# Cross-attention and quantised FFN on one core: less filler, other orders in the opening and the tail, two DMAs swapped

## The chip, the core and the metric

The kernel runs on one core of one Trainium2 chip, in one launch. The metric is the device time of that launch in microseconds. Five engines run side by side, each with its own instruction queue, and order each other by semaphores: TensorE (PE, matmuls; its weight loads are shown as PEld), VectorE (DVE), ScalarE (ACT), GpSimd (POOL) and SyncE (SP, which here only issues DMAs). Matmul results go to PSUM, which the kernel cuts into eight banks of 128 x 512 floats. All times below are microseconds unless marked ns.

## The reference, cut to what matters

```python
def layernorm(x): m = mean(x, -1); v = var(x, -1); return (x - m) / sqrt(v + 1e-5)

# x: (8, 56, 128), ctx: (8, 1500, 96); 8 heads of 64
q = (layernorm(x) @ Wq).reshape(b, n, 8, 64)
k = (ctx @ Wk).reshape(b, m, 8, 64);  v = (ctx @ Wv).reshape(b, m, 8, 64)
attn = softmax(einsum('bihd,bjhd->bhij', q, k) * 64 ** -0.5, -1)
x = x + einsum('bhij,bjhd->bihd', attn, v).reshape(b, n, 512) @ Wout + bout

def act_quant(x, clip): s = sigmoid(clip) * max(abs(x)) / 127; return clip(round(x / s), -128, 127) * s
def weight_quant(w):    s = max(abs(w), axis=1) / 127;         return clip(round(w / s), -128, 127) * s
h = layernorm(x);  xq = act_quant(h, clip_x)           # one scale for all of x
gate, up = xq @ weight_quant(w_gate).T, xq @ weight_quant(w_up).T      # 352 wide
h = act_quant(silu(gate) * up, clip_down)              # one scale for all of h
out = x + h @ weight_quant(w_down).T
```

## The kernel before

**Algebra and tiling.** The 8 x 56 tokens stand as 4 pairs of batches, 112 tokens each. For each head Wq and Wk are multiplied first (`weights_qk`, four products of two heads each), so that a query has 96 values and meets the context directly; Wv and Wout likewise. Scores are computed transposed: 125 keys by 448 queries (8 heads of 56 tokens), 12 key tiles to a batch, so 96 iterations n in all. To keep float32 accuracy with the fast matmul type, each operand is split in a high part (`_hi`) and a rest (`_lo`): the scores of a tile are three matmuls (`scores_lo` two, `scores_hi` one), and the weighted sum is three more (`weighted`), three iterations later (LAG = 3).

**Maxima.** The softmax subtracts an estimate of the maximum of each query's scores. It comes from the high parts alone: four groups (G = 4) of 112 queries against three pieces of 500 keys, so twelve chunk matmuls a batch, each followed by a VectorE maximum. The maximum goes in as a 97th row of `q_hi` against a row of -1 in `ctxT_hi`; that row is what `max_moved` counts, 16 for each of the four groups. For batch b+1 the chunks are spread over the iterations of batch b by `chunks_at`: from t = 0 to 9 the chunks 2 to 11, and at t = 10 and 11 the chunks 0 and 1 of batch b+2. For batches 1 to 7 SyncE moves the four rows by DMA (`move_max`, L243). For batch 0 the rows are transposed by small matmuls (`row`, L1136) into PSUM and copied by ScalarE (`row_copy`, L473), two groups at a time.

**The opening (L961 to L1185 on PE).** Seven filler matmuls of 512 columns, then the weight products of the first quarter, filler, the transpose of the first 112 tokens (which waits for `xn0_made`), filler, and then for each of the four groups g: two query matmuls (`first_queries`, L1141), their copy by ScalarE into `q_hi` and, in full precision, into `e_full` (`split_first_q`, L443, for groups 0 and 1; one line each for the others, L468 and L471), three chunk matmuls (`first_max_chunks`, L990) and one VectorE maximum over 1500 keys (`first_max`, L659). The banks of the chunks alternate between `p_m` and `p_n`, so group g also waits for the maximum of group g-2. The other three token pairs are normalised meanwhile, two by ScalarE (`normalised`, L455) and one by GpSimd (L319), transposed (L1168), and copied as `xnT`. The queries of heads 0 to 3 of batches 2 to 7 (`query`, L1119) stand ahead of iteration 0, those of heads 4 and 5 in iteration 0, of 6 in 1, of 7 in 2 (`LOOP_QUERIES`). Each uses the bank named in `q_banks` (L164), which must first be free: head 6 shares `p_o[1]` with head 4, head 7 shares `p_mb[1]` with head 3. ScalarE copies a query out (L483), VectorE subtracts to get `q_lo` (L668), and that frees the bank.

**Filler.** `busy(n, bank, cols)` (L963) issues n bf16 matmuls of `cols` columns on zeros, whose result nobody reads.

**DMA queues.** SyncE issues the first token pair (`x_in` pair 0), weight quarter 0, the first context in three pieces, and later all contexts. ScalarE issues the other three token pairs (L435) and weight quarter 1 (L436). VectorE has the statistics of the three pairs (L633) ahead of the rest of the first normalisation (L637 to L644) in its queue.

**The tail.** After the last weighted sum: normalise, project, second layer norm (L866 to L902), quantise x, gate and up products, quantise h, down product. The last pair's centring is ScalarE's L573; it waits for `shift2`. h has three row blocks f: VectorE quantises and casts f = 0 and 2 (L944 to L951), ScalarE f = 1 (L610, L613). The down product has one bank for each half of the tokens; each takes three matmuls, f = 0, 1, 2.

Of the kernel before, what the change touches and what calls it, by code (L numbers as in the profile page):

```python
# [4 lines left out]
F32 = mybir.dt.float32  # L5
# [42 lines left out]
def chunks_at(b, t):  # L48
    if t >= T - 2:
        return [(b + 2, t - (T - 2))] if b + 2 < B else []  # L50
    if b + 1 >= B:
        return []
    if b == 0:
        return [(1, c) for c in range(sum(FIRST_CHUNK_PLAN[:t]), sum(FIRST_CHUNK_PLAN[:t + 1]))]
    return [(b + 1, t + 2)]
# [6 lines left out]
def program(nc, x_d, ctxT_d, ctx_d, wqkT_d, wvT_d, wout_d, misc_d, wg_d, wu_d, wd_d, out_d):  # L62
    stack = ExitStack()
    with stack:
# [99 lines left out]
        q_banks = [p_s[1], p_s[0], p_mb[0], p_mb[1], p_o[1], p_mb[2], p_o[1], p_mb[1]]  # L164
        qk_banks = [p_s, p_nb[0:2], p_s, p_s]
        first_q = [bank[0:C, 2 * TOK * k:2 * TOK * (k + 1)] for bank in (p_x, p_s[1]) for k in range(2)]
        row_banks = [p_s[0], p_mb[2]]
# [66 lines left out]
        def _(sp):  # L234
# [23 lines left out]
            for p in range(1, 3):  # L258
                sp.dma_start(ctxT_hi[p][C:C + 1, :].bitcast(F32), ctxT_hi[0][C:C + 1, :].bitcast(F32)).then_inc(s.minus_copied, 16)
            wait_ctxT_lo(sp, 0)  # L260
# [27 lines left out]
        def _(pool):  # L288
# [36 lines left out]
            pool.wait_ge(s.first_q_full_made, 3)  # L325
# [105 lines left out]
        def _(act):  # L431

            act.wait_ge(s.warm_made, 1)
            act.activation(warm[:, :], warm[:, :], ACT.Exp)
            act.dma_start(x_in[:, 1:PAIRS, :], x_d[:, 1:PAIRS, :]).then_inc(s.x_loaded, 16)  # L435
            act.dma_start(wqkT[:, 1, :], wqkT_d[:, 1, :]).then_inc(qk_loaded[1], 16)  # L436
# [27 lines left out]
            normalised(1)  # L464
            normalised(2)
            act.wait_ge(s.first_q_made, G)
            for g in range(2, G):
                act.activation(pair0(q_hi, slice(2 * g, 2 * g + 2)), by_batch(first_q[g]), ACT.Copy).then_inc(s.first_q_hi_made, 1)  # L468
            act.wait_ge(s.xnT_made, 2)
            act.activation(xnT[:, TOK:ALLTOK], p_s[0][:, 0:ALLTOK - TOK], ACT.Copy, scale=-0.5).then_inc(s.xnT_copied, 1)  # L470
            act.activation(pair0(e_full, slice(4, H)), by_batch(p_s[1][0:C, 0:HQ]), ACT.Copy).then_inc(s.first_q_full_made, 1)  # L471

            def row_copy(k):  # L473

                cols = slice(2 * k * GQ, 2 * (k + 1) * GQ)
                act.wait_ge(s.row_made, k + 1)
                act.activation(q_hi[C:C + 1, 0, cols], row_banks[k][C:C + 1, cols], ACT.Copy).then_inc(max_moved[0], 32)
# [17 lines left out]
            row_copy(0)  # L495
            split_q(0)
            split_q(1)
            row_copy(1)
# [120 lines left out]
        def _(dve):  # L619
# [200 lines left out]
            for b in range(B):  # L820
# [53 lines left out]
                .then_inc(s.late_x_made, 1)  # L874
            dve.wait_ge(s.projected, PAIRS - 1)
# [3 lines left out]
            dve.wait_ge(s.ln2_step, 2 * PAIRS - 2)  # L879
            dve.tensor_scalar(veps2[:, :], mv2[:, 1:2], EPS, None, ALU.add).then_inc(s.veps2_made, 1)  # L880
            dve.tensor_scalar(shift2[:, :], mv2[:, 0:1], -0.5, None, ALU.mult).then_inc(s.shift2_made, 1)
            dve.wait_ge(s.late_x_made, 1)
            dve.reduce_max(late_max[:, :], late_x[:, :], AX.X, apply_absolute_value=True).then_inc(s.late_step, 1)
# [63 lines left out]
            dve.wait_ge(s.h_step, 3)  # L947
            dve.tensor_copy(hq[:, 0, :], h8[:, 0, :]).then_inc(s.h_quantised, 1)
            dve.wait_ge(s.h_step, 4)
            for cols in HALVES:  # L950
                dve.tensor_copy(hq[0:96, 2, cols], h8[0:96, 2, cols]).then_inc(s.h_quantised, 1)  # L951
# [10 lines left out]
        def _(pe):  # L962
# [21 lines left out]
            busy(5, p_x, 128)  # L984
# [3 lines left out]
            busy(9, p_x, 128)  # L988

            def first_max_chunks(g, pieces=range(NM)):  # L990
# [4 lines left out]
                for k in pieces:  # L995
# [7 lines left out]
            def max_chunk(b, c):  # L1003
# [6 lines left out]
                if b == 1 and c < 3:  # L1010
                    pe.wait_ge(s.last_q_lo_made, (1, 6, 4)[c])
# [107 lines left out]
            def query(h):  # L1119

                if h == 0:
                    pe.wait_ge(s.first_q_full_made, 3)
                elif h == 1:
                    pe.wait_ge(max_moved[0], 32)
                elif h < 4:
                    pe.wait_ge(s.first_max_made, G - 1)
                elif h == 4:
                    pe.wait_ge(s.first_max_made, G)
                elif h == 6:
                    pe.wait_ge(s.last_q_lo_made, 3)  # L1130
                elif h == 7:
                    pe.wait_ge(s.last_q_lo_made, 2)
# [3 lines left out]
            def row(g):  # L1136

                return pe.matmul(row_banks[g // 2][C:C + 1, g * GQ:(g + 1) * GQ], maxima[0][:, g:g + 1], ident[0:GQ, 0:GQ],
                                 start=True, stop=True)
# [12 lines left out]
            first_max_chunks(0, (0,))  # L1152
            busy(3, p_s[0], 128)
            first_max_chunks(0, (1,))
# [3 lines left out]
            first_max_chunks(0, (2,))  # L1158
# [5 lines left out]
            first_queries(3)  # L1164
            pe.wait_ge(s.xn_made, 2)
# [4 lines left out]
            first_max_chunks(2)  # L1170
            first_max_chunks(3)
            pe.wait_ge(s.xnT_copied, 2)
            row(0)
            row(1).then_inc(s.row_made, 1)
# [91 lines left out]
            pe.wait_ge(s.h_quantised, 1)  # L1266
            for k, cols in enumerate(HALVES):
                pe.matmul(y_banks[k][:, 0:ALLTOK // 2], wdT[:, 0, :], hq[:, 0, cols], start=True, stop=False)
            for k, cols in enumerate(HALVES):
                pe.wait_ge(s.h1_quantised, k + 1)  # L1270
                pe.matmul(y_banks[k][:, 0:ALLTOK // 2], wdT[:, 1, :], hq[:, 1, cols], start=False, stop=False)
                pe.wait_ge(s.h_quantised, k + 2)
# [46 lines left out]
```

## Time and profile before

| | us |
|---|---|
| median of 3 runs | 181.56 (181.48 to 181.96) |
| the profiled execution's own time | 181.43 |
| its span in the trace | 179.4 |
| busy: PE, PEld, DVE, ACT, POOL | 172.7, 142.6, 144.7, 133.8, 127.8 |
| opening, up to the first exponential of the loop (L534) | 17.43 |
| from the last matmul of the loop to the end of the last issue | 160.8 to 177.6 |

The span is the time between the first and the last thing that the hardware profiler recorded on the core; the profiled execution's own time is measured from outside and is 2.0 longer. Busy time of PE includes the filler and overlaps of pipelined matmuls, whose ends are modelled. In the timeline an entry is the start, the length, the engine, the line of the code with its operation, output and inputs and shapes, how many are merged (x3), and in brackets how long the engine was idle before it and which engine, tile and line ended that.

### The profile page before, as it was taken

How to read it: one execution, taken by the hardware profiler on the slowest of the kernel's cores; microseconds unless marked ns; L12 is line 12 of the kernel's file. 1: busy time of each engine (PE TensorE's matmuls, PEld its weight loads, DVE VectorE, ACT ScalarE, POOL GpSimd, SP SyncE). 2: the span in 40 equal slices, each digit the busy share in tenths (PEclk: the TensorE clock that was granted, in tenths of full speed). 3: DMA queues.
4: the chain of work that ended last, by engine and by line, in shares of the span. 5: the costliest groups of instructions: out<-in, count | busy, mean ns of one | idle time of the engine just before them, and what ended most of it. 6: DMA issues, size and time to landing. Idle time of an engine off the chain costs nothing.

```text
span 179.4 us, 2941 instructions
## 1 busy us (share of the span) xinstructions
PE 172.7 (96%) x889; PEld 142.6 (79%) x889; DVE 144.7 (81%) x341; ACT 133.8 (75%) x284; POOL 127.8 (71%) x135
## 2 busy tenths in 40 slices
PE   7999999999999999999999999999999999999783
PEld 2865678888888889888888898888888888898431
DVE  6596578969984896899987968999979869958784
ACT  3477989878869995778878857788877677855732
POOL 5698399989995888689987866899788675533010
PEclk9999999999999999999999999999999999999999
DMA  5767900180017000800071008100400000000001
GB/s 151 224 167 214 257 27 4 13 242 8 0 44 213 0 4 2 249 5 2 0 215 45 2 0 230 31 0 0 130 0 2 4 0 0 0 0 5 0 0 51
DMA packets 8331, 11.41 MB, mean 64 GB/s; under 512 B 4276, under 2 KB 6516, under 8 KB 8316
## 3 DMA queue, kind: packets, MB, share of 16 engines
q1 hardware_dynamic: 7900, 10.83, 22.8%
q10 hardware_dynamic: 416, 0.40, 0.7%
q8 instruction: 7, 0.11, 0.3%
q14 instruction: 8, 0.07, 0.1%
HBM read 10.97 MB, written 0.23 MB: 62 GB/s over the span
## 4 chain that ended last, share of the span: by engine, by line
PE 91%; DVE 5%; ACT 1%; issue 1%; DVEq 0%; POOL 0%; ACTq 0%; POOLq 0%
PE p_n L1057 11%; PE p_sw L1038 11%; PE p_m L1016 11%; PE p_n L1065 11%; PE p_sw L1030 11%; PE p_n L1059 11%; PE p_sw L1031 11%; PE p_n L966 2%; PE p_n L1073 1%; PE p_n L1093 1%; PE p_m L1133 1%; DVE h_flat L924 1%; PE p_m L1000 1%; PE p_n L1000 1%; PE p_sw L1133 1%
## 5 line engine op out<-in xcount | busy, mean ns | idle before, releaser
L370 POOL TENSOR_TENSOR e_lo<-e_full,e_hi 125x448 fp32r<-125x448 f32 x48 | 55.7, 1160 | 26.0 <-ACT e_full L537 24.8
L534 ACT ACTIVATE e_hi<-p_sw 125x448 fp32r<-125x448 f32 x96 | 52.2, 543 | 23.9 <-PE p_sw L1038 23.3
L675 DVE TENSOR_REDUCE chunk_max<-p_m 112x1 f32<-112x500 f32 x84 | 55.6, 673 | 16.3 <-PE p_m L1016 15.4
L1030 PE MATMUL p_sw<-q_hi,ctxT_lo 96*125 96x448 f32 x96 | 36.3, 378 | 0.0
L1057 PE MATMUL p_n<-e_hi,ctx_hi 125*128 125x448 f32 x96 | 35.5, 370 | 0.0
L1038 PE MATMUL p_sw<-q_hi,ctxT_hi 97*125 97x448 f32 x96 | 35.4, 369 | 0.0
L1065 PE MATMUL p_n<-e_lo,ctx_hi 125*128 125x448 f32 x96 | 35.1, 366 | 0.0
L1031 PE MATMUL p_sw<-q_lo,ctxT_hi 96*125 96x448 f32 x96 | 35.1, 365 | 0.0
L1059 PE MATMUL p_n<-e_hi,ctx_lo 125*96 125x448 f32 x96 | 35.0, 364 | 0.0
L690 DVE TENSOR_TENSOR e_lo<-p_n,e_hi 125x448 fp32r<-125x448 f32 x48 | 29.6, 617 | 4.0 <-ACT p_n L551 3.8
L1016 PE MATMUL p_m<-ctxT_hi,q_hi 96*112 96x500 f32 x84 | 32.2, 393 | 0.0
L348 POOL TENSOR_TENSOR ctxT_lo<-ctxT_in,ctxT_hi 96x500 fp32r<-96x500 f32 x21 | 26.6, 1266 | 1.6
L551 ACT ACTIVATE p_n<-p_sw 125x448 f32<-125x448 f32 x48 | 25.8, 537 | 2.0 <-DVE e_lo L690 1.6
L537 ACT ACTIVATE e_full<-p_sw 125x448 f32<-125x448 f32 x48 | 25.9, 539 | 0.0
L358 POOL TENSOR_TENSOR ctx_lo<-ctx_in,ctx_hi 125x384 fp32r<-125x384 f32 x24 | 24.2, 1010 | 1.9
L1065 PEld LDWEIGHTS p_n<-e_lo,ctx_hi 125*128 125x128 f32 x96 | 18.0, 188 | 4.1
L1057 PEld LDWEIGHTS p_n<-e_hi,ctx_hi 125*128 125x128 f32 x96 | 18.2, 190 | 2.7
L1031 PEld LDWEIGHTS p_sw<-q_lo,ctxT_hi 96*125 96x125 f32 x96 | 18.0, 188 | 2.1
L1038 PEld LDWEIGHTS p_sw<-q_hi,ctxT_hi 97*125 97x125 f32 x96 | 17.8, 185 | 1.8
L1030 PEld LDWEIGHTS p_sw<-q_hi,ctxT_lo 96*125 96x125 f32 x96 | 17.8, 185 | 1.8
L1059 PEld LDWEIGHTS p_n<-e_hi,ctx_lo 125*96 125x96 f32 x96 | 15.7, 163 | 3.3
L1016 PEld LDWEIGHTS p_m<-ctxT_hi,q_hi 96*112 96x112 f32 x84 | 14.8, 177 | 2.2 <-ACT ctxT_hi L491 0.4
(255 smaller groups left out, 206.2 us busy)
## 6 DMA issues: line engine op xcount, KB each, us to landing
ctx_in<-ctx_d SPq DMA_DIRECT2D x8, 504.0 KB
ctxT_in<-ctxT_d SPq DMA_DIRECT2D x7, 562.5 KB, 5.9
ctxT_in<-ctxT_d SPq DMA_DIRECT2D x3, 187.5 KB, 4.4
ctx_in<-ctx_d SPq DMA_DIRECT2D x8, 58.5 KB
q_hi<-maxima SPq DMA_DIRECT2D x28, 0.4 KB, 1.9
wout<-wout_d SPq DMA_DIRECT2D x1, 256.0 KB, 7.4
wqkT<-wqkT_d SPq DMA_DIRECT2D x1, 224.0 KB, 4.4
wvT<-wvT_d SPq DMA_DIRECT2D x1, 192.0 KB, 6.7
```

Source lines behind the costliest of these rows:

```text
L348: pool.tensor_tensor(ctxT_lo[b % 2][:, key_piece(k)], ctxT_in[b % 2][:, key_piece(k)], ctxT_hi[b % 3][0:C, key_piece(k)], ALU.subtract).th ...
L370: pool.tensor_tensor(e_lo[:, k, :], e_full[:, k, :], e_hi[:, k, :], ALU.subtract)\
L534: act.activation(e_hi[:, k, :], p_s[n % 2][0:KT, 0:HQ], ACT.Exp, scale=SCALE)\
L675: dve.reduce_max(chunk_max[:, c // NM, c % NM:c % NM + 1], p_mb[c % NM][0:GQ, 0:MC], AX.X)\
L690: dve.tensor_tensor(e_lo[:, k, :], p_x[0:KT, 0:HQ], e_hi[:, k, :], ALU.subtract).then_inc(s.lo_dve_made, 1)
L1016: pe.matmul(p_mb[k][0:GQ, 0:MC], q_hi[0:C, b, g * GQ:(g + 1) * GQ], ctxT_hi[b % 3][0:C, key_piece(k)], start=True, stop=True).then_inc(s.m ...
L1030: pe.matmul(o, ctxT_lo[b % 2][:, keys], q_hi[0:C, b, :], start=True, stop=False)
L1031: pe.matmul(o, ctxT_hi[b % 3][0:C, keys], q_lo[:, b, :], start=False, stop=False)
L1038: pe.matmul(p_s[n % 2][0:KT, 0:HQ], ctxT_hi[b % 3][:, t * KT:(t + 1) * KT], q_hi[:, b, :], start=False, stop=True)\
L1057: pe.matmul(o[:, 0:HQ], ctx_hi[b % 2][:, t, :], e_hi[:, k, :], start=(t == 0), stop=False, skip_group_check=True)
L1059: pe.matmul(o[0:C, 0:HQ], ctx_lo[b % 2][:, t, :], e_hi[:, k, :], start=False, stop=False, skip_group_check=True)
L1065: pe.matmul(o[:, 0:HQ], ctx_hi[b % 2][:, t, :], e_lo[:, k, :], start=False, stop=(t == T - 1), skip_group_check=True).then_inc(s.pv_done, 1)
```

## The change

It touches the following places:

- `chunks_at`: for batch 6, which has no batch 8 to prepare, the chunks of batch 7 run from t = 0 (two of them) to t = 8.
- `q_banks`: heads 6 and 7 swap banks, with their waits in `query` and in `max_chunk`. 
- `first_q`: groups 2 and 3 are in banks of their own (`p_s[0]` and `p_s[1]`) rather than both in `p_s[1]`.
- The rows of groups 0 and 1 of batch 0 are moved by two DMAs on SyncE's queue; `row` and `row_copy` do only groups 2 and 3.
- ScalarE's queue issues weight quarter 1 ahead of x; after the first normalisation it copies group 2, and after the second group 3.
- PE: 3 filler matmuls rather than 5, 5 rather than 9, and the 3 between the chunks of group 0 are gone; the third chunk of group 0 is ahead of the queries of group 1; the chunks of group 2 are ahead of the transposes, which now wait for `first_q_full_made` 3, since they write the bank of group 2.
- Tail on VectorE: `late_max` ahead of the last statistics, `shift2` ahead of `veps2`; the casts of h by halves of the tokens, f = 0 and 2 alternately, and PE's down product one half after the other.

```diff
return [(1, c) for c in range(sum(FIRST_CHUNK_PLAN[:t]), sum(FIRST_CHUNK_PLAN[:t + 1]))]
+    if b == B - 2:
+        return [(b + 1, c) for c in ((2, 3) if t == 0 else (t + 3,) if t + 3 < CHUNKS else ())]
     return [(b + 1, t + 2)]
...
         p_o, p_x = p_nb[0:2], p_nb[2]
-        q_banks = [p_s[1], p_s[0], p_mb[0], p_mb[1], p_o[1], p_mb[2], p_o[1], p_mb[1]]
+        q_banks = [p_s[1], p_s[0], p_mb[0], p_mb[1], p_o[1], p_mb[2], p_mb[1], p_o[1]]
         qk_banks = [p_s, p_nb[0:2], p_s, p_s]
-        first_q = [bank[0:C, 2 * TOK * k:2 * TOK * (k + 1)] for bank in (p_x, p_s[1]) for k in range(2)]
-        row_banks = [p_s[0], p_mb[2]]
+        first_q = [bank[0:C, 2 * TOK * k:2 * TOK * (k + 1)] for bank, k in ((p_x, 0), (p_x, 1), (p_s[0], 0), (p_s[1], 0))]
         g0_banks = [p_x, p_o[1]]
...
                 sp.dma_start(ctxT_hi[p][C:C + 1, :].bitcast(F32), ctxT_hi[0][C:C + 1, :].bitcast(F32)).then_inc(s.minus_copied, 16)
+            for g in range(G - 2):
+                sp.wait_ge(s.first_max_made, g + 1)
+                sp.dma_start(q_hi[C:C + 1, 0, g * GQ:(g + 1) * GQ].bitcast(F32), maxima[0][:, g:g + 1])\
+                    .then_inc(max_moved[0], 16)
             wait_ctxT_lo(sp, 0)
...
                                    ALU.subtract).then_inc(s.first_ctxT_lo_made, 1)
-            pool.wait_ge(s.first_q_full_made, 3)
+            pool.wait_ge(s.first_q_full_made, G)
...
             act.activation(warm[:, :], warm[:, :], ACT.Exp)
+            act.dma_start(wqkT[:, 1, :], wqkT_d[:, 1, :]).then_inc(qk_loaded[1], 16)
             act.dma_start(x_in[:, 1:PAIRS, :], x_d[:, 1:PAIRS, :]).then_inc(s.x_loaded, 16)
-            act.dma_start(wqkT[:, 1, :], wqkT_d[:, 1, :]).then_inc(qk_loaded[1], 16)
...
             act.wait_ge(s.shift_made, 1)
-            normalised(1)
-            normalised(2)
-            act.wait_ge(s.first_q_made, G)
             for g in range(2, G):
-                act.activation(pair0(q_hi, slice(2 * g, 2 * g + 2)), by_batch(first_q[g]), ACT.Copy).then_inc(s.first_q_hi_made, 1)
+                normalised(g - 1)
+                split_first_q(g)
             act.wait_ge(s.xnT_made, 2)
             act.activation(xnT[:, TOK:ALLTOK], p_s[0][:, 0:ALLTOK - TOK], ACT.Copy, scale=-0.5).then_inc(s.xnT_copied, 1)
-            act.activation(pair0(e_full, slice(4, H)), by_batch(p_s[1][0:C, 0:HQ]), ACT.Copy).then_inc(s.first_q_full_made, 1)
-            def row_copy(k):
-                cols = slice(2 * k * GQ, 2 * (k + 1) * GQ)
-                act.wait_ge(s.row_made, k + 1)
-                act.activation(q_hi[C:C + 1, 0, cols], row_banks[k][C:C + 1, cols], ACT.Copy).then_inc(max_moved[0], 32)
+            def row_copy():
+                act.wait_ge(s.row_made, 1)
+                act.activation(q_hi[C:C + 1, 0, 2 * GQ:HQ], p_mb[2][C:C + 1, 2 * GQ:HQ], ACT.Copy).then_inc(max_moved[0], 32)
...
             ctxT1_hi(0)
-            row_copy(0)
             split_q(0)
             split_q(1)
-            row_copy(1)
+            row_copy()
             split_q(2)
...
                 .then_inc(s.late_x_made, 1)
+            dve.wait_ge(s.late_x_made, 1)
+            dve.reduce_max(late_max[:, :], late_x[:, :], AX.X, apply_absolute_value=True).then_inc(s.late_step, 1)
             dve.wait_ge(s.projected, PAIRS - 1)
...
             dve.wait_ge(s.ln2_step, 2 * PAIRS - 2)
+            dve.tensor_scalar(shift2[:, :], mv2[:, 0:1], -0.5, None, ALU.mult).then_inc(s.shift2_made, 1)
             dve.tensor_scalar(veps2[:, :], mv2[:, 1:2], EPS, None, ALU.add).then_inc(s.veps2_made, 1)
-            dve.tensor_scalar(shift2[:, :], mv2[:, 0:1], -0.5, None, ALU.mult).then_inc(s.shift2_made, 1)
-            dve.wait_ge(s.late_x_made, 1)
-            dve.reduce_max(late_max[:, :], late_x[:, :], AX.X, apply_absolute_value=True).then_inc(s.late_step, 1)
             dve.wait_ge(s.late_pow, 2)
...
                 dve.tensor_scalar(h8[0:fn, f, :], hh[0:fn, f, 0:ALLTOK], hs[0:fn, 2:3], None, ALU.mult).then_inc(s.h_step, 1)
-            dve.wait_ge(s.h_step, 3)
-            dve.tensor_copy(hq[:, 0, :], h8[:, 0, :]).then_inc(s.h_quantised, 1)
             dve.wait_ge(s.h_step, 4)
             for cols in HALVES:
-                dve.tensor_copy(hq[0:96, 2, cols], h8[0:96, 2, cols]).then_inc(s.h_quantised, 1)
+                for f in (0, 2):
+                    fn = FT[f][1]
+                    dve.tensor_copy(hq[0:fn, f, cols], h8[0:fn, f, cols]).then_inc(s.h_quantised, 1)
             dve.tensor_tensor(hs[:, 0:1], hs[:, 1:2], wscale[:, 6:7], ALU.mult).then_inc(s.y_step, 1)
...
             weights_qk(0).then_inc(s.wqk_made, 1)
-            busy(5, p_x, 128)
+            busy(3, p_x, 128)
             pe.wait_ge(s.ident_made, 2)
...
             pe.transpose(p_mb[2][:, 0:TOK], xn[:, 0, :], ident[0:TOK, 0:TOK]).then_inc(s.xnT_made, 1)
-            busy(9, p_x, 128)
-            def first_max_chunks(g, pieces=range(NM)):
+            busy(5, p_x, 128)
+            def first_max_chunks(g):
...
                     pe.wait_ge(s.first_max_made, g - 1)
-                for k in pieces:
+                for k in range(NM):
                     if g == 1 and k == 2:
...
                 if b == 1 and c < 3:
-                    pe.wait_ge(s.last_q_lo_made, (1, 6, 4)[c])
+                    pe.wait_ge(s.last_q_lo_made, (1, 5, 4)[c])
                 done = CHUNKS * (b - 1) + c - NM + 1
...
                 if h == 0:
-                    pe.wait_ge(s.first_q_full_made, 3)
+                    pe.wait_ge(s.first_q_full_made, G)
                 elif h == 1:
-                    pe.wait_ge(max_moved[0], 32)
+                    pe.wait_ge(s.xnT_copied, 2)
                 elif h < 4:
...
                     pe.wait_ge(s.first_max_made, G)
-                elif h == 6:
-                    pe.wait_ge(s.last_q_lo_made, 3)
-                elif h == 7:
-                    pe.wait_ge(s.last_q_lo_made, 2)
+                elif h >= 6:
+                    pe.wait_ge(s.last_q_lo_made, h - 4)
                 pe.matmul(q_banks[h][0:C, TOK:ALLTOK], wqk[:, h % 2, h // 2, :], xnT[:, TOK:ALLTOK], start=True, stop=True)\
...
-                return pe.matmul(row_banks[g // 2][C:C + 1, g * GQ:(g + 1) * GQ], maxima[0][:, g:g + 1], ident[0:GQ, 0:GQ],
+                return pe.matmul(p_mb[2][C:C + 1, g * GQ:(g + 1) * GQ], maxima[0][:, g:g + 1], ident[0:GQ, 0:GQ],
                                  start=True, stop=True)
...
             busy(2, p_s[0], 128)
-            first_max_chunks(0, (0,))
-            busy(3, p_s[0], 128)
-            first_max_chunks(0, (1,))
+            first_max_chunks(0)
             pe.wait_ge(s.wqk_copied, 2)
...
             first_queries(1)
-            first_max_chunks(0, (2,))
             weights_qk(2)
...
             first_queries(3)
+            first_max_chunks(2)
+            pe.wait_ge(s.first_q_full_made, 3)
             pe.wait_ge(s.xn_made, 2)
...
             last.then_inc(s.xnT_made, 1)
-            first_max_chunks(2)
             first_max_chunks(3)
             pe.wait_ge(s.xnT_copied, 2)
-            row(0)
-            row(1).then_inc(s.row_made, 1)
             query(0)
...
-            pe.wait_ge(s.h_quantised, 1)
             for k, cols in enumerate(HALVES):
+                pe.wait_ge(s.h_quantised, 2 * k + 1)
                 pe.matmul(y_banks[k][:, 0:ALLTOK // 2], wdT[:, 0, :], hq[:, 0, cols], start=True, stop=False)
-            for k, cols in enumerate(HALVES):
                 pe.wait_ge(s.h1_quantised, k + 1)
                 pe.matmul(y_banks[k][:, 0:ALLTOK // 2], wdT[:, 1, :], hq[:, 1, cols], start=False, stop=False)
-                pe.wait_ge(s.h_quantised, k + 2)
+                pe.wait_ge(s.h_quantised, 2 * k + 2)
                 pe.matmul(y_banks[k][:, 0:ALLTOK // 2], wdT[0:96, 2, :], hq[0:96, 2, cols], start=False, stop=True)\
...
```

## Rows read from the trace of the kernel before

**Rows 1.** The page, busy time of each engine
```profile
PE 172.7 (96%) x889; PEld 142.6 (79%) x889; DVE 144.7 (81%) x341; ACT 133.8 (75%) x284; POOL 127.8 (71%) x135
```

**Rows 2.** Chain of waits, 0 to 17.5: start, us, engine, tile, line
```profile
5.60 0.62 PE p_n L966 x9
6.22 0.42 PE p_n L1144 x4
6.64 0.40 PE p_n L980 x4
...
8.40 0.23 PE p_m L1000
8.63 0.62 PE p_sw L980 x8
9.25 0.86 PE p_n L1000 x3
```

**Rows 3.** Timeline, 0 to 14: start, us, engine, line, shapes, [idle before <-releaser]
```profile
3.57 0.68 DVE L633 BATCH_NORM_STATS2 stats<-x_in 112x6 f32<-112x128 f32 x3 [0.21 <-DMA x_in<-x_in_d]
...
4.63 0.34 DVE L644 TENSOR_SCALAR xn<-x_in,mv,rstd 112x128 f32<-112x128 f32 x1
...
5.63 0.26 ACT L451 ACTIVATE xnT<-p_m 128x112 f32<-128x112 f32 x1 [0.50 <-PE p_m L987]
...
8.67 1.72 DVE L663 TENSOR_REDUCE maxima<-p_m 112x1 f32<-112x1500 f32 x1 [1.23 <-PE p_m L1000]
...
9.69 0.87 ACT L456 ACTIVATE xn<-x_in,nt,rstd 112x128 f32<-112x128 f32 x2
...
10.92 0.60 ACT L468 ACTIVATE q_hi<-p_sw 96x224 fp32r<-96x224 f32 x2 [0.37 <-PE p_sw L1144]
...
12.29 1.72 DVE L663 TENSOR_REDUCE maxima<-p_m 112x1 f32<-112x1500 f32 x1 [0.27 <-PE p_m L1000]
...
13.93 1.71 DVE L663 TENSOR_REDUCE maxima<-p_n 112x1 f32<-112x1500 f32 x1
```

**Rows 4.** DMAs: issue in the timeline, then KB and us to landing
```profile
0.92 0.39 ACTq L435 DMA_DIRECT2D x_in<-x_in_d  x1
...
1.35 0.44 ACTq L436 DMA_DIRECT2D wqkT<-wqkT_d  x1
...
q_hi<-maxima SPq DMA_DIRECT2D x28, 0.4 KB, 1.9
...
x_in<-x_in_d ACTq DMA_DIRECT2D x1, 168.0 KB, 2.6
...
wqkT<-wqkT_d ACTq DMA_DIRECT2D x1, 112.0 KB, 2.8
```

**Rows 5.** Groups by shape, filler weight loads at 4.9 and 5.9: mean ns
```profile
L966 PEld LDWEIGHTS p_n<-filler 128*128 128x128 bf16 x2 | 0.3, 152 | 0.0
...
L966 PEld LDWEIGHTS p_n<-filler 128*128 128x128 bf16 x3 | 0.2, 98 | 0.0
```

**Rows 6.** Timeline, 17 to 25, and a window (PE, PEld, DVE, ACT, POOL)
```profile
17.00 0.92 DVE L668 TENSOR_TENSOR q_lo<-p_m,q_hi 96x336 fp32r<-96x336 f32 x2 [1.36 <-ACT q_hi L483]
...
18.77 0.36 PE L1038 MATMUL p_sw<-q_hi,ctxT_hi 97*125 97x448 f32 x1
...
19.33 0.81 PE L1133 MATMUL p_n<-xnT,wqk 128*96 128x336 f32 x2 [0.20 <-DVE q_lo L668]
...
24.96 0.27 PEld L1016 LDWEIGHTS p_m<-ctxT_hi,q_hi 96*112 96x112 f32 x2 [0.36 <-ACT ctxT_hi L491]
...
21.00:23.00 2.00, 2.00 (x10) 1.65 (x9) 1.98 (x4) 2.00 (x6) 1.09 (x1) 1.00 0.92 237
```

**Rows 7.** Chain, then timeline, of the tail
```profile
165.52 0.07 DVE shift L881
...
175.64 0.45 DVE L951 CAST hq<-h 96x224 bf16<-96x224 int8 x2
...
176.44 0.81 DVE L957 SCALAR_TENSOR_TENSOR y<-p_n,hs,x1T 128x224 f32<-128x224 f32 x2 [0.28 <-PE p_n L1273]
```

## The prediction

> **What bounds the kernel now.** I read the page's busy line first: TensorE (PE) is busy 96% of the span [rows 1]. That alone says little, since filler matmuls count. The chain of waits of the opening says more [rows 2]: it stays on PE from the first filler to the loop, and nine filler matmuls stand in it just ahead of the first queries. The timeline of VectorE and ScalarE in that stretch gives the second line of work [rows 3]: four maxima of 1.72 us each, the last starting at 13.93 and so ending at 15.64, with one gap of 0.27 before the third. After it PE still runs the last row, one query and the first scores. In the loop matmuls follow each other at about 0.2 us, so the loop's length doesn't move with a shift of its start, except in its first iterations [rows 6]. In the tail every step is a dependency [rows 7].
>
> So the time moves by three things: when the fourth maximum ends, stalls in iterations 0 to 5, and steps of the tail.
>
> **Opening: the load order.** Now x is issued at 0.92 and lands 2.6 later, at 3.52; the weight quarter is issued at 1.35 and lands 2.8 later, at 4.15 [rows 4]. VectorE, idle until then, takes the three statistics at 3.57, and everything of the first normalisation stands behind them in its queue (xn0 is computed at 4.63 to 4.97) [rows 3]. Swapped, x is issued at 1.35. Bounds: it keeps its 2.6 and lands 0.43 later, or it takes the place of the second transfer (same bytes in total) and lands 0.63 later. I take 0.6. Nobody waits for the weight quarter's earlier arrival: its products come after the first queries, at 6.6. So this edit alone is a loss. The Trainium skill, DMA: Bandwidth & Descriptors, section on queues, rings and completion order, says that on each DMA engine descriptors are consumed in ring order and that ScalarE's queue is one row of rings. By that rule x would wait for the weights' bytes, the sum would go by 0.63, and the row pair above agrees in order, though no run here shows the swap.
>
> **Opening: less filler.** xn0 at 5.57 instead of 4.97. The copy of the transposed block starts 0.66 after xn0 now, with five fillers in front of the transpose; with three, and PE long free, I take 0.5: copy at 6.07 instead of 5.63, done at 6.33 [rows 3]. Before, the nine fillers held PE to 5.60+0.62=6.22 and only then came the queries [rows 2]. With five they end before 6.33, so the queries start near 6.45: the 0.6 loss has become 0.25. From there, by the chain's own pieces: queries 0.42, weight products 0.40, two fillers 0.2 (nine make 0.62), and three chunks of maxima at 0.23 each, now in one piece, without three fillers and without the second queries between: 6.45+0.42+0.40+0.2+0.69=8.16. The first maximum would start at about 8.25 instead of 8.67: gain 0.4.
>
> **Opening: the maxima.** They run at a spacing of 1.64 when fed. Second: VectorE is free at 8.25+1.64=9.9; PE, done with the chunks at 8.2, does queries 0.4, weight products 0.62 and chunks 0.86: 10.1. So 10.1 instead of 8.67+1.64=10.31. Third: now it starts at 12.29, and what it waited for is q_hi, copied only after both normalisations (9.69, 0.87 long) and after both query groups (10.92) [rows 3]. With the copy between the normalisations and only one group waited for, ScalarE can copy at about 10.5, when PE has done the third group's queries (10.1+0.42). From this copy to the maximum it takes 1.37 (10.92 to 12.29): 11.87; VectorE is free at 10.1+1.64=11.75. PE does the fourth group's queries in between, till 10.95, where the copy ends too. Gain 0.4. Fourth: 13.5 to 15.2, if its chunks are ready: the transposes now wait for the third group's full copy and the second normalisation, done by ScalarE at about 11.6 (q_hi, full copy and one normalisation from 10.5), then three transposes, which I put at the 0.4 of four query matmuls, then chunks like the 0.86: 12.9. Behind this new wait on PE stand the fourth group's chunks and all late queries, 0.6 ahead of need. If the cover goes, each 0.1 costs 0.1.
>
> **Opening: rows by DMA.** Two rows go from PE and ScalarE to SyncE's queue: four small matmuls and a 0.35 copy less, two transfers more. They wait for the first and second maxima (ending at 8.25+1.72=10.0 and 11.8); such a transfer lands 1.9 after issue [rows 4], at 13.7, and is needed by the first full scores, after the fourth maximum (15.2): hidden, with 1.5 us to spare. Behind these waits in SyncE's queue are the loads of the next context, which wait for GpSimd's ctxT_lo anyway: cost 0. The remaining row copy stays after the last maximum. GpSimd's own chain moves with x, and the first scores wait for it too; it has its q_lo well before the fourth maximum ends now, and I put it at 0. If it came last, the cost would be what x is late less the 0.4, some 0.2 more.
>
> From the end of the fourth maximum all is as before: opening -0.4, bounds 0 and -1.0 (x not late at all: first maximum at 7.6, PE-fed chain after it).
>
> **Loop, iterations 0 to 5.** The seventh query waits for the bank of the fifth: PE starts the last scores of iteration 1 at 18.77, 0.2 long, and the query only at 19.33, when the fifth's q_lo is done [rows 6]. The new bank is freed by the fourth query's q_lo (17.00+0.92), so that 0.36 of PE goes; what is late next is ScalarE, which is busy for all of 21 to 23 and releases the chunk at 24.96 after 0.36 of waiting. Its last pause before that was for scores that stood behind the stalled query, so it restarts about 0.4 earlier too. The chunk of iteration 4 also waits for one query less. Gain 0.45, bounds 0 (ScalarE late for another reason) and 0.6.
>
> **Batch 6.** Its chunks come one iteration earlier, as many as before. The last row lands just in time for batch 7 now and 1.4 earlier then; PE shows no gap there. VectorE gets one maximum earlier, with iterations of slack. 0, bounds -0.1 and +0.1.
>
> **Tail.** shift2 issued before veps2: the chain gives that place 0.07, and ScalarE's centring follows it at 165.62 [rows 7]; GpSimd's power gets its input 0.07 later and is then just in time for the Newton step. The earlier late_max (0.28) fits before the statistics at 164.82, or overhangs by up to 0.1. Net -0.05. Quantising: the first y matmuls wait for a half cast, not a whole one, but that cast must now wait for both h8 pieces; four casts at a spacing of 0.19 instead of one whole and two halves. The hs product, behind the casts on VectorE, moves from 176.01 to about 176.2 and lets the first y start near 176.40 instead of 176.44. -0.05, bounds -0.15 and +0.15.
>
> **Sum.** The profiled execution took 181.43 (span 179.4 and 2.0 around). -0.4-0.45-0.1=-0.95: 180.48. The median 181.56 is 0.13 above the profiled one: 180.6. No change can be told from measurement within 0.3%, 0.54 us, so faster means under 181.02.
>
> **Rivals.**
> A, x is hardly late: it lands early enough through the busier first transfers that its 0.6 loss vanishes. For it: the 2.6 and 2.8 differ little. Against: it is the longer transfer and goes second. Opening -0.95 instead of -0.4: 180.05. Chance 0.17.
> B, one of the two main gains is not there: x is late by 1 us, or a matmul group, a copy on ScalarE or its restart takes the place of what is removed. For it: PE, ScalarE and VectorE are all within 0.1 to 0.5 of each other at the second, third and fourth maximum. Time 181.0 to 181.3. Chance 0.22.
> C, slower: PE's clock stays at its low level longer. The granted clock column reads 1.00 throughout, but weight loads of the filler take 152 ns around 4.9 and 98 around 5.8, in the same shape [rows 5]; I read that as the rise from 1.2 to 2.4 GHz, at about 5.6, after PE had been busy without a gap. With two fillers less and x late, PE stands idle from about 5.1 to 5.6. If the rise is missed, the 1.73 of matmuls up to the first maximum and much of the 1.0 after it double: first maximum at about 10, fourth ending at 16.6, +1.0 instead of -0.4: 182.0, and 182.5 if the third and fourth groups are slow too. It decides from the point where the filler's weight loads still read 150 ns after 6. Against: the rise came after nearly five microseconds of work, of which this takes half of one. Chance 0.11, half of it beyond 182.1.
> The Trainium skill, TensorE: Matmul & The Clock Gate, section on the clock gate, says the default state is throttled and activity releases the throttle; this is the rule by which C would come. The rise in the fillers' loads agrees with it.
>
> Forecast's own case 0.50, range 180.2 to 181.0. Whole range 179.9 to 181.6: it takes in A, B and leaves out C. Faster 0.50+0.17+a fifth of B, less some of my own spread: 0.68; same 0.25; slower 0.07.
>
> **What would show it.** x's statistics start near 4.15 instead of 3.57 (A: 3.6 to 3.8). First maximum at 8.25, fourth ends at 15.2; the gap before the third is under 0.1. No wait of a query for q_lo in iteration 1; ScalarE restarts at 0.4 more than the opening's shift. Centring 0.07 closer to the statistics before it; y at the same distance from the cast. Wrong would be: the fourth maximum ending at 15.6 or later, filler loads of 150 ns after 6, a PE gap on the moved rows, or a new wait on ScalarE between 18 and 25 that gives the seventh query's gain back.

## The result, and the profile after

The changed kernel takes 185.18 us (median of 5 executions, 184.6 to 185.43), before 181.56: ratio 1.0192, 95% interval 1.0175 to 1.0208. So it is slower by 3.6 us where 1.0 less was forecast. The profiled execution, the fastest of the five, took 184.6; its span is 182.4.

Busy time and the granted clock of the page, in 40 slices of 4.56 us each:

```profile
PE 174.6 (96%) x875; PEld 145.3 (80%) x876; DVE 144.9 (79%) x342; ACT 133.5 (73%) x284; POOL 127.7 (70%) x135
...
PEclk9756999999999999999999999999999999999999
```

The second, third and fourth slice read 7, 5 and 6 where the kernel before has 9: somewhere from 5 to 18 us the clock was near half. The table by windows is sharper. Its columns are the stretch, its length with PE's busy time, then PEld, DVE, ACT and POOL, the granted clock, the share of the DMA engines and GB/s:

```profile
4.00:5.00 1.00, 0.58 (x7) 0.31 (x7) 0.60 (x4) 0.33 (x1) 0.22 (x1) 1.00 0.93 268
5.00:6.00 1.00, 0.08 (x1) 0.11 (x2) 0.93 (x7) 0.00 (x0) 0.00 (x0) 1.00 1.08 299
...
7.00:8.00 1.00, 1.00 (x8) 0.62 (x7) 0.42 (x1) 0.60 (x2) 0.84 (x3) 0.51 0.68 126
...
10.00:11.00 1.00, 1.00 (x9) 0.78 (x9) 1.00 (x1) 0.53 (x2) 1.00 (x2) 0.50 0.98 288
...
15.00:17.00 2.00, 2.00 (x8) 1.50 (x7) 1.13 (x1) 0.88 (x4) 1.54 (x2) 0.50 0.30 39
...
19.00:21.00 2.00, 2.00 (x11) 1.26 (x11) 0.63 (x2) 1.73 (x5) 0.88 (x1) 1.00 0.95 222
```

Half speed, 1.2 GHz, holds from 7 on (finer windows put its ends at 7.0 and 17.2). Before it PE did nearly nothing between 4.6 and 5.9 (it was busy for 0.58 and 0.08 of the first two windows). The timeline of the opening, to be read against [rows 3] and [rows 4]:

```profile
1.34 0.44 ACTq L441 DMA_DIRECT2D x_in<-x_in_d  x1
...
3.84 0.30 PEld L980 LDWEIGHTS p_sw<-wqkT 64*128 64x128 f32 x4 [0.66 <-DMA wqkT<-wqkT_d]
...
4.23 0.17 PEld L966 LDWEIGHTS p_n<-filler 128*128 128x128 bf16 x3
...
4.40 0.68 DVE L633 BATCH_NORM_STATS2 stats<-x_in 112x6 f32<-112x128 f32 x3 [0.90 <-DMA x_in<-x_in_d]
...
5.43 0.34 DVE L644 TENSOR_SCALAR xn<-x_in,mv,rstd 112x128 f32<-112x128 f32 x1
...
5.89 0.14 PEld L987 LDWEIGHTS p_m<-ident,xn 112*128 112x128 f32 x1 [1.49 <-issue]
5.92 0.29 PE L987 MATMUL p_m<-ident,xn 112*128 112x112 f32 x1 [1.34 <-DVE xn L644]
...
8.04 0.92 PEld L1000 LDWEIGHTS p_m<-ctxT_hi,q_hi 96*112 96x112 f32 x3
...
9.72 1.72 DVE L663 TENSOR_REDUCE maxima<-p_m 112x1 f32<-112x1500 f32 x1 [2.30 <-PE p_m L1000]
...
13.09 1.72 DVE L663 TENSOR_REDUCE maxima<-p_n 112x1 f32<-112x1500 f32 x1 [1.65 <-PE p_n L1000]
...
15.87 1.72 DVE L663 TENSOR_REDUCE maxima<-p_m 112x1 f32<-112x1500 f32 x1 [1.06 <-PE p_m L1000]
...
17.57 1.72 DVE L663 TENSOR_REDUCE maxima<-p_n 112x1 f32<-112x1500 f32 x1
```

Two lines of the kernel before, for comparison:

```profile
4.01 0.51 PEld L980 LDWEIGHTS p_sw<-wqkT 64*128 64x128 f32 x4 [0.84 <-DMA wqkT<-wqkT_d]
...
9.18 0.50 PEld L1000 LDWEIGHTS p_n<-ctxT_hi,q_hi 96*112 96x112 f32 x3
```

x now lands 0.83 later (statistics at 4.40 against 3.57). PE has loaded its last filler weights by 4.4 and its next weight load comes at 5.89, 1.49 later; its matmuls end at 4.6, so that it is itself idle for 1.34 (the bracket of its own line). The brackets of weight loads below read longer than PE's own waits in the same way. The three weight loads of the first chunks then take 0.92 together, where three of the same shape take 0.50 in the kernel before. The loads of the weight products show the level earlier still: 0.30 for four at 3.84, where the kernel before has 0.51 at 4.01. So here the clock had already risen, and fell again. The four maxima start at 9.72, 13.09, 15.87 and 17.57, not at 8.67, 10.31, 12.29 and 13.93: between them VectorE waits for chunks at half speed.

From there on the kernel is faster than before. The first exponential, the seventh query (22.62, at once after the scores of iteration 1), and the tail:

```profile
21.08 0.54 ACT L534 ACTIVATE e_hi<-p_sw 125x448 fp32r<-125x448 f32 x1
...
22.42 0.36 PE L1038 MATMUL p_sw<-q_hi,ctxT_hi 97*125 97x448 f32 x1
...
22.62 0.73 PE L1131 MATMUL p_m<-xnT,wqk 128*96 128x336 f32 x2
...
163.98 0.42 DVE L731 STREAM_TRANSPOSE den_t<-p_n 32x224 f32<-32x224 f32 x1 [0.82 <-PE p_n L1065]
...
168.51 0.15 DVE L882 TENSOR_SCALAR shift<-mv 112x1 f32<-112x1 f32 x1
...
168.70 0.37 ACT L573 ACTIVATE x_now<-p_n,shift 112x128 f32<-112x128 f32 x1 [1.07 <-DVE shift L882]
...
178.53 0.83 DVE L951 CAST hq<-h 128x224 bf16<-128x224 int8 x4
...
179.46 0.81 DVE L957 SCALAR_TENSOR_TENSOR y<-p_n,hs,x1T 128x224 f32<-128x224 f32 x2
```

| stretch | before | after | difference |
|---|---|---|---|
| start to first exponential (L534) | 17.43 | 21.08 | +3.65 |
| to the first step of the last normalisation (L731) | 143.41 | 142.90 | -0.51 |
| to the start of y (L957) [rows 7] | 15.60 | 15.48 | -0.12 |
| sum, against the spans 179.4 and 182.4 | | | +3.02 |

Many of these kernels have two groups of times, and the ratios below leave out an execution that is more than 1.5% above its kernel's fastest, so beside each ratio I give the groups. I call a time over 182.4 upper. The kernel before has 7 upper times in 90 executions (182.89 to 186.43); the others lie at 181.1 to 182.1.

### The profile page after: what moved, and what is told of

The parts are those of the page before. It is cut to its first block, busy times and chain, and to the rows that moved or that the text cites. A ratio compares the mean times of both kernels' runs of the same rounds, so it can differ in the third digit from the quotient of the medians.

```text
span 182.4 us, 2915 instructions
## 1 busy us (share of the span) xinstructions
PE 174.6 (96%) x875; PEld 145.3 (80%) x876; DVE 144.9 (79%) x342; ACT 133.5 (73%) x284; POOL 127.7 (70%) x135
## 4 chain that ended last, share of the span: by engine, by line
PE 85%; DVE 7%; ACT 4%; DMA 2%; issue 1%; DVEq 0%; POOL 0%; ACTq 0%; POOLq 0%
PE p_n L1057 11%; PE p_n L1065 10%; PE p_n L1059 10%; PE p_m L1016 10%; PE p_sw L1038 10%; PE p_sw L1030 10%; PE p_sw L1031 10%; DMA x_in<-x_in_d 2%; PE p_n L1000 1%; PE p_n L1073 1%; PE p_m L1000 1%; PE p_m L1131 1%; DVE h_flat L924 1%; ACT e_hi L534 1%; PE p_sw L1142 1%
## 5 line engine op out<-in xcount | busy, mean ns | idle before, releaser
L534 ACT ACTIVATE e_hi<-p_sw 125x448 fp32r<-125x448 f32 x96 | 52.3, 544 | 23.6 <-PE p_sw L1038 23.1
```

What stands on the lines that cost most here:

```text
L534: act.activation(e_hi[:, k, :], p_s[n % 2][0:KT, 0:HQ], ACT.Exp, scale=SCALE)\
```

## The experiments

Theory 1: PE has nothing to do for over a microsecond while it waits for x, and that costs the clock. Theory 2: the nine or so fillers less cost it, whenever x comes. Theory 3: it isn't the clock but the new order of PE's opening.

**The changed kernel, x first again.**

```diff
-act.dma_start(wqkT[:, 1, :], ...)
 act.dma_start(x_in[:, 1:PAIRS, :], ...)
+act.dma_start(wqkT[:, 1, :], ...)
```

> The changed kernel with x first again on ScalarE's queue; everything else stays, the lesser filler too. Theory 1 (the half clock from 7.0 to 17.2 comes from PE's idle time between 4.6 and 5.9, and that from x landing 0.8 later): the idle time shrinks to about 0.5, the granted clock stays 1.00, first maximum at 7.8 to 8.3, time 180.0 to 180.8. Theory 2 (nine fillers less are enough to lose the clock, whenever x comes): a stretch at 0.50 in the opening and 183.5 to 185. Theory 3 (not the clock but the new order of PE's opening costs the time): 184 or more at full clock.

Measured: 180.14, ratio 0.9930 (0.9909 to 0.9951); 6 executions, none upper. Timeline:

```profile
5.30 0.14 PEld L987 LDWEIGHTS p_m<-ident,xn 112*128 112x128 f32 x1 [0.37 <-issue]
...
8.30 1.72 DVE L663 TENSOR_REDUCE maxima<-p_m 112x1 f32<-112x1500 f32 x1 [0.57 <-PE p_m L1000]
...
13.58 1.71 DVE L663 TENSOR_REDUCE maxima<-p_n 112x1 f32<-112x1500 f32 x1
```

The wait before the transpose is 0.37, the loads are of full speed, the fourth maximum starts at 13.58. Theory 3 falls at this place, and theory 2 as it was put (whenever x comes): the same order and the same lesser filler give a kernel faster than before by 1.3 us. One number is odd: the granted clock reads 0.95 from between 5 and 6 us on in this profile. Its loop is only 0.26 longer than in the run with both back (143.13 against 142.87 from the first exponential to L731), where 5% would be 7, so I don't read it as a speed.

**The changed kernel, filler of 5 and 9 back, x second.**

```diff
-busy(3, p_x, 128)
+busy(5, p_x, 128)
 ...
-busy(5, p_x, 128)
+busy(9, p_x, 128)
```

> The changed kernel with 5 and 9 fillers again around the first transpose; x stays second on ScalarE's queue. PE is still idle for about 1.1 before the transpose, since two fillers more last 0.2. Theory 1 (the idle time for x decides): the half clock stays, 184 to 185.5. Theory 2 (the number of fillers decides): the clock is kept, 181.0 to 181.5. Theory 3 (order of PE's opening): 184 or more at full clock.

Measured: median 181.00 of 10, ratio 0.9973 (0.9946 to 0.9999). Six lie at 180.62 to 181.04, four are upper, 182.52 to 185.78. The profile caught one of 182.52:

```profile
6.22 0.18 PEld L987 LDWEIGHTS p_m<-ident,xn 112*128 112x128 f32 x1 [1.07 <-issue]
...
9.13 0.83 PEld L1000 LDWEIGHTS p_m<-ctxT_hi,q_hi 96*112 96x112 f32 x3
...
11.32 0.49 PEld L1000 LDWEIGHTS p_n<-ctxT_hi,q_hi 96*112 96x112 f32 x3
```

Each theory had expected one group; it is both. The wait is 1.07 (0.84 of PE itself), and here the clock did not fall but rose late: three chunk loads take 0.83 at 9.1 and 0.49 at 11.3. With x second the filler does count: four upper times of 10 with 5 and 9 fillers, and 15 of 17 with 3 and 5 (the first five and the twelve further down).

**The changed kernel, both back.**

> The changed kernel with x first and with 5 and 9 fillers again; the new orders, banks, rows by DMA and tail stay. Theories 1 and 2 alike: full clock, 180.2 to 180.9 (opening -0.3 to -0.6, iterations 0 to 5 -0.5, tail -0.1). Theory 3: 184 or more at full clock.

Measured: 180.22, ratio 0.9928 (0.9905 to 0.9951), 4 executions, none upper.

```profile
3.53 0.68 DVE L633 BATCH_NORM_STATS2 stats<-x_in 112x6 f32<-112x128 f32 x3 [0.19 <-DMA x_in<-x_in_d]
...
8.07 1.72 DVE L663 TENSOR_REDUCE maxima<-p_m 112x1 f32<-112x1500 f32 x1 [0.58 <-PE p_m L1000]
...
13.35 1.71 DVE L663 TENSOR_REDUCE maxima<-p_n 112x1 f32<-112x1500 f32 x1
...
16.85 0.54 ACT L534 ACTIVATE e_hi<-p_sw 125x448 fp32r<-125x448 f32 x1
```

The opening is 0.58 shorter than before (16.85 against 17.43). This is what the new orders are worth with x early and the clock kept.

**The kernel before, only the two DMAs swapped.**

> The kernel before with only the two DMAs on ScalarE's queue swapped; all its filler stays. x lands 0.8 later and PE is idle for about 0.7 before the first transpose. Theory 1 with a sharp limit on idle time below 0.7: half clock, 185 to 186. Theory 1 with more tolerance, and theory 2: only the delay itself, 181.9 to 182.3. If the swap is harmless altogether: 181.4 to 181.7.

Measured: median 182.08 of 10, ratio 1.0027 (1.0013 to 1.0041). Seven lie at 181.91 to 182.11, three are upper, at 186.19, 186.95 and 188.36. The profile is of the lower group:

```profile
6.00 0.14 PEld L987 LDWEIGHTS p_m<-ident,xn 112*128 112x128 f32 x1 [1.29 <-issue]
...
18.15 0.54 ACT L534 ACTIVATE e_hi<-p_sw 125x448 fp32r<-125x448 f32 x1
```

At full clock the swap costs what it delays: the first exponential comes 0.72 later (18.15 against 17.43). The rest is the chance of an upper time: 3 of 10 with the swap alone and all filler in place, against 0 of 21 for the kernel before beside it. These are few executions, and the three upper ones have no profile. The one profiled kept its clock with PE idle for 1.15.

**The changed kernel once more.**

> The changed kernel once more, unchanged, for the spread of its times. Two kernels with x second have given two groups of times each (filler back: 180.6 to 181.0 and 182.5 to 185.8; only swapped: 181.9 to 182.1 and 186.2 to 188.4), both kernels with x first only one. Theory 1 (the idle time before the transpose can cost the clock, by the moment at which it falls): two groups here too, one near 180.6 and one at 184.5 to 185.5, the upper one in over half of the executions. Rival (this kernel always loses the clock): all at 184.5 to 185.5.

Measured: median 184.67 of 12: two at 180.86 and 180.91, ten upper from 182.77 to 186.23. Its ratio of 1.0028 (0.9976 to 1.0079) rests on five of the twelve, the two and the three at 182.77 to 183.53, and leaves the seven slowest out; the median is 3.0 above that of the kernel before beside it (181.66). With the first five, 15 of 17 are upper. The profile of one at 184.74:

```profile
4.02 0.51 PEld L980 LDWEIGHTS p_sw<-wqkT 64*128 64x128 f32 x4 [0.84 <-DMA wqkT<-wqkT_d]
...
5.75 0.18 PEld L987 LDWEIGHTS p_m<-ident,xn 112*128 112x128 f32 x1 [0.82 <-issue]
5.79 0.42 PE L987 MATMUL p_m<-ident,xn 112*128 112x112 f32 x1 [0.58 <-DVE xn L644]
...
8.37 0.91 PEld L1000 LDWEIGHTS p_m<-ctxT_hi,q_hi 96*112 96x112 f32 x3
...
16.34 0.78 PEld L1000 LDWEIGHTS p_n<-ctxT_hi,q_hi 96*112 96x112 f32 x3
```

Here the low level holds from the start: the weight products load at the low rate (0.51 for four, 0.30 in the first profile after), and so do the chunks at 8.4 and at 16.3 (0.91 and 0.78). The granted clock column of the trace reads 1.00 for all of it. So there are two ways into the same loss: a clock that had risen and falls, and one that doesn't rise. PE's own idle time was only 0.58 here: at the low level the products and the filler ended at 5.20 and not at 4.59, and x came a little earlier (4.26). So theory 1's "over a microsecond" is too narrow.

**The kernel before, only the lesser filler.**

> The kernel before with only the lesser filler: 3 for 5, 5 for 9, and the 3 between the chunks of group 0 gone; x first. Theory 1: PE's idle time stays under 0.6, no time of the upper kind, and as two of these fillers hold up the queries by some 0.1, 181.2 to 181.6. Theory 2 (the filler itself decides): some times at 184 and more.

Measured: median 181.23 of 10, ratio 0.9967 (0.9942 to 0.9993): nine at 180.96 to 181.40, one at 185.66. By the medians the filler taken out gives 0.4 (181.23 against 181.66), and one upper time in ten is no more than the kernel before can have. In the profiled execution the first weights came late, PE was idle for 0.88 before them, and the loads behind that gap are at full speed (0.30 for four, at 4.78).

**The changed kernel, 16 fillers ahead of the transpose, x second.** This changes nothing but what PE does while it waits.

```diff
-busy(3, p_x, 128)
+busy(16, p_x, 128)
```

> The changed kernel, x second, with 16 fillers of 128 columns in place of the 3 ahead of the transpose, so that PE works while it waits for x. Theory 1: no time of the upper kind, all at 180.6 to 181.2 (x's delay of 0.4 to 0.8 stays). Rival (x's late arrival costs by itself, through DMA or VectorE, and not by the clock): some or all at 184 and more. If the bridge is too long at the low level it costs up to 0.6 in some executions.

Measured: 180.92, ratio 0.9954 (0.9932 to 0.9976). Twelve executions, all at 180.65 to 181.33, none upper.

```profile
4.43 0.68 DVE L633 BATCH_NORM_STATS2 stats<-x_in 112x6 f32<-112x128 f32 x3 [0.86 <-DMA x_in<-x_in_d]
4.49 0.94 PEld L966 LDWEIGHTS p_n<-filler 128*128 128x128 bf16 x16
...
5.92 0.14 PEld L987 LDWEIGHTS p_m<-ident,xn 112*128 112x128 f32 x1 [0.49 <-issue]
...
8.69 1.72 DVE L663 TENSOR_REDUCE maxima<-p_m 112x1 f32<-112x1500 f32 x1 [0.99 <-PE p_m L1000]
...
17.45 0.54 ACT L534 ACTIVATE e_hi<-p_sw 125x448 fp32r<-125x448 f32 x1
```

x lands as late as in the changed kernel (4.43 against 4.40); the wait is 0.49 and not 1.49; the loss is gone. 15 upper of 17 against 0 of 12, from thirteen matmuls whose result nobody reads. PE's own idle time is 0.34 here. The rival that x's lateness costs the 3.6 by itself falls: for itself it costs 0.3 to 0.6, the distance of the first exponential to those of the four profiles of the changed kernel with x first and seven fillers at the start (16.85 to 17.15). Of the twelve timed beside these twelve, ten were upper. The thirteen matmuls fill the gap and are also more work in it; no run tells these two apart.

**The kernel before, only the banks of heads 6 and 7.**

> The kernel before with only the banks of heads 6 and 7 swapped and their waits. The prediction's term: -0.36 to -0.5, 181.0 to 181.15, with the third exponential about 0.4 closer to the first than in the kernel before (3.36). Rival (ScalarE takes the place of the stall): 181.4 to 181.6.

Measured: median 181.22 of 12, ratio 0.9984 (0.9949 to 1.0018): ten at 180.88 to 181.55, two upper. By the times alone this is unclear, since the ratio still holds the two upper ones (183.07 and 183.5). The trace has it:

```profile
17.64 0.54 ACT L534 ACTIVATE e_hi<-p_sw 125x448 fp32r<-125x448 f32 x1
...
20.62 0.53 ACT L534 ACTIVATE e_hi<-p_sw 125x448 fp32r<-125x448 f32 x1
...
160.59 0.42 DVE L731 STREAM_TRANSPOSE den_t<-p_n 32x224 f32<-32x224 f32 x1 [0.82 <-PE p_n L1065]
```

Third exponential 2.98 after the first, where the kernel before has 20.79-17.43=3.36; first exponential to last normalisation 142.95 against 143.41. That is -0.46, the forecast term.

**x first, 8 fillers ahead of the transpose; and both back once more.**

> The changed kernel with x first and 8 fillers ahead of the transpose (3 in the changed kernel), 5 after it: PE has no idle time there even when x lands some tenths later. Theory 1: one group of times, 180.0 to 180.4, below the kernel before by 1.1 to 1.5. If 8 fillers are too many at the low level: 180.3 to 180.6.

Measured: 180.55, ratio 0.9953 (0.9924 to 0.9982), one upper of 10.

> The kernel with x first and with 5 and 9 fillers again, all else as changed, once more for its spread: 180.1 to 180.6, at most one or two of twelve in the upper group, as in the kernel before (4 of 61).

Measured: 180.63, ratio 0.9952 (0.9930 to 0.9975), one upper of 12, at 185.44, and one at 182.15. By the medians the two are 1.0 and 0.9 under the kernel before, timed beside them (181.57). The first time both back had been 1.3 under it (180.22 against 181.48). The kernel with x first and the lesser filler stays the fastest, at 180.14. It was not timed beside these two, so that order isn't shown.

**Both back, 4 instead of 7 fillers at the start.**

```diff
-busy(7, p_x)
+busy(4, p_x)
```

> The same kernel as the last with x first and all its filler, but only 4 instead of 7 fillers of 512 columns at the very start: PE has nothing to do from about 2.6 to 4.0, and nobody waits for it then. Theory 1 (an idle stretch of over 1 us in the opening, wherever it lies, makes a long low level likely): an upper group at 183 to 186 in half of the executions or more. Rival (the loss belongs to x's late arrival and the transpose): one group, 180.1 to 180.4.

Measured: median 184.33 of 12: three at 181.13 to 181.44, one at 182.36, eight upper up to 184.63. The ratio 1.0007 (0.9968 to 1.0045) leaves out seven of the eight, 184.26 to 184.63. The profile, of one at 182.81:

```profile
5.45 0.50 PEld L980 LDWEIGHTS p_sw<-wqkT 64*128 64x128 f32 x4 [3.55 <-DMA wqkT<-wqkT_d]
5.45 0.74 PE L980 MATMUL p_sw<-wqkT 64*128 64x96 f32 x4 [2.65 <-DMA wqkT<-wqkT_d]
...
9.49 0.67 PEld L1000 LDWEIGHTS p_m<-ctxT_hi,q_hi 96*112 96x112 f32 x3
...
11.52 0.50 PEld L1000 LDWEIGHTS p_n<-ctxT_hi,q_hi 96*112 96x112 f32 x3
```

x is early here and the filler before the transpose is whole. PE's gap lies at another place, after the last 512-column filler, and the upper group is there again: the chunk loads take 0.67 at 9.5 and 0.50 at 11.5, so the low level lasted to between the two. In this execution the weight quarter also landed late, so PE was idle for 2.65 (2.8 to 5.45) and not for the 1.4 I had reckoned. Its first exponential, at 19.39, therefore holds that delay too; what the weights did in the executions at 184.3 to 184.6 no profile shows. So the loss isn't bound to x, the transpose or the swap as such: it also comes with a stretch without PE work at another place in the first microseconds.

PE's own longest idle time in each profile (from the first filler to the first maximum), beside the upper times of its kernel:

| kernel | idle | TensorE's clock in that profile | upper times |
|---|---|---|---|
| changed, first profile | 1.34 | risen by 3.84, low from 7.0 to 17.2 | 15 of 17, with the next row |
| changed, second profile | 0.58 | low to 17 | |
| changed, 4 fillers at the start, both back | 2.65 | rises after 9.5 | 8 of 12 |
| changed, 5 and 9 fillers | 0.84 | rises after 9.1 | 4 of 10 |
| before, swapped | 1.15 | kept | 3 of 10 |
| before, less filler | 0.88 | high behind the gap | 1 of 10 |
| changed, 16 fillers | 0.34 | kept | 0 of 12 |
| the other five, x first (six profiles) | 0.15 at most | risen by about 6.3 | 11 of 134 |

The four kernels whose order leaves PE without work in the opening have 30 upper times of 49, all the others 12 of 156. In a single execution the length alone doesn't tell which way the clock goes: the low level stayed with 0.58, and the clock was high after 0.88 and 1.15.

## Why the prediction was wrong

**The step that failed** is the price and the chance of the clock: "C, slower: PE's clock stays at its low level longer", with "Chance 0.11" and "182.0, and 182.5 if the third and fourth groups are slow too". It was the likeliest case: 15 of 17 executions. Its price was mis-sized as well: half speed over about ten microseconds of the opening gives +3.65 to the first exponential (+3.63 against the same kernel with the clock kept, 21.08 against 17.45), where I had let it double the matmuls up to the second maximum for +1.0, and +1.5 with the third and fourth groups. The forecast itself held the clock's term at nothing.

**What led there** is the gap. "PE stands idle from about 5.1 to 5.6" was 4.6 to 5.9. Two terms of it were off: x landed 0.83 late and not 0.6 (the upper bound was 0.63; the runs with x second show statistics at 4.26 to 4.73, those with x first at 3.44 to 3.72), and fillers and weight products take little more than half as long when the clock has risen early (weight loads 0.30 against 0.51 for four), so PE was done sooner, at 4.6. But the length of the gap is not all of it: in the second profile of the changed kernel PE was idle for 0.58, from 5.2 to 5.8, nearly the half microsecond that I had put, and the rise was missed all the same. My reason for the small chance was that of nearly five microseconds of work "this takes half of one"; so little was enough. I counted the filler as a thing that holds up the queries, and for a gain. That it held the clock I gave one case in nine. The Trainium skill, TensorE: Matmul & The Clock Gate, section on the clock gate, says that the default is throttled and activity releases it. The pair of runs with 3 and 16 fillers agrees with it in direction, 15 upper times of 17 and 0 of 12; it doesn't say how often the release is missed.

**Late x, for itself.** I had put "the 0.6 loss has become 0.25" and a gain of 0.4 for the opening. With the clock kept (16 fillers) the first maximum starts at 8.69 and not 8.25, and the first exponential at 17.45: a gain of 0.0. With x first it is 0.58 (0.28 to 0.58 over four profiles). So the swap costs 0.3 to 0.6 here, and 0.72 in the kernel before, with nothing to set against it, as the prediction said in kind. The forecast gain of 0.4 for the opening is what x first gives, and not this kernel.

**Order of the opening.** Right in kind: with x first the first maximum starts at 8.07 (8.30 with the lesser filler) and the fourth 5.28 later. I had 5.25, since the gap before the third goes and one before the second comes; before it is 5.26. So all of the gain is the earlier first maximum. Neither the new wait ahead of the transposes nor the moved rows showed as a wait.

**Iterations 0 to 5.** Right: -0.45 forecast, -0.51 in the changed kernel, -0.46 with the banks alone. The working read the last scores at 18.77 as 0.2 long to get a stall of 0.36; the row [rows 6] shows 0.36 long and 0.20 idle. The third exponential came 0.38 closer to the first, so what was removed is nearer to the 0.36.

**Tail.** Right: -0.1 forecast, -0.12. The centring follows 4.72 after the start of the tail against 4.78, and from the reduction that gives the scale of h (L939) to y it is 2.31 against 2.36.

**Batch 6.** Forecast 0; no run separates it. The loop's -0.51 against -0.46 leaves at most some hundredths.

In the lower group the number would have held, though not by all of its terms: the two lower executions of the changed kernel are 180.86 and 180.91, the twelve with 16 fillers 180.65 to 181.33, and 180.6 was forecast. They are 0.7 to 0.8 under the kernel before beside them, from the loop and the tail; the opening gave none of its 0.4. No profile shows one of the two, so that they kept the clock is argued from the kernel with 16 fillers.

## What to carry to other kernels

Before filler is taken out, or work that feeds the first matmuls is moved later, add up PE's longest gap in the first microseconds, with the durations of the high level too, since they make it longer. Gaps of 0.6 to 1.3 there cost more here than every reordering gained, and such a gap can show as a spread of times before it shows as a median (4 of 10 and 3 of 10 above): time such a change often enough to see both groups. Judge the level by the length of a weight load of known shape; the clock column can read 1.00 throughout, as in the second profile of the changed kernel.

## What the runs showed of the hardware that was not expected

- The low level can last ten microseconds in the midst of dense matmuls: 7.0 to 17.2 in the first profile after, with PE busy in all of it.
- The clock can rise by 3.84, before the first product (loads of 0.30 for four), and fall again at 7.0, after a gap from 4.6 to 5.9; or not rise at all till 17. Which of them happens differs between executions of one kernel. What decides it is open; in the swapped kernel PE was idle for 1.15 in the execution of 182.08 and kept its clock.
- The same transfer lands at quite different moments: x as the second DMA is first used between 4.26 and 4.73, and the first weight quarter, loaded by PE at 3.84 to 4.09 in most runs, at 4.78 in the run with less filler and at 5.45 in the one with the early gap.
- In one execution the granted clock reads 0.95 from somewhere between 5 and 6 us on, past the end of the loop, though its loop is only 0.26 longer than another's at 1.00.
